# LoRA-conditioned routing kernel on one core: nine warm-ups, W's opening in halves, a full-width bias sum, the last batch by halves with its last chunks stored singly, and one product moved up

## What is computed

```python
def cond(x, adapter_mapping, W, b, lora_As, lora_Bs):      # R = 16, SCALING = 2
    base_out = jnp.einsum('bti,oi->bto', x, W) + b
    A, Bm = lora_As[adapter_mapping], lora_Bs[adapter_mapping]
    lora_h = jnp.einsum('bti,bir->btr', x, A)
    return base_out + jnp.einsum('btr,bro->bto', lora_h, Bm) * SCALING

def ffn(x, route_w, A, Bw):                                # E = 8 experts, R = 16
    logits = jnp.einsum('bsd,ed->bse', x, route_w)
    topk_v, topk_idx = jax.lax.top_k(logits, 1)
    route_weight = jax.nn.one_hot(topk_idx[..., 0], E) * topk_v
    wh = route_weight[..., None] * jnp.einsum('bsd,erd->bser', x, A)
    return jnp.einsum('bser,eor->bso', wh, Bw)

out = x + ffn(cond(x, ...), route_w, A, Bw)
```

## Time and profile before

| | us |
|---|---|
| median of 3 runs | 292.27 |
| lowest, highest | 291.97, 293.33 |
| the profiled execution | 293.44 |
| its span in the trace | 291.64 |

### The profile page before, as it was taken

How to read it: one execution, slowest core, us unless ns; L and a number is a source line. 1 busy time by engine, 2 the same in 40 slices (tenths; PEclk the granted TensorE clock), 3 DMA queues, 4 the chain that set the end, 5 groups by cost and what they waited for, 6 DMA issues and landing times.

```text
span 291.6 us, 4476 instructions
## 1 busy us (share of the span) xinstructions
PE 284.0 (97%) x1731; PEld 228.1 (78%) x1731; DVE 203.5 (70%) x238; ACT 113.3 (39%) x171; POOL 12.7 (4%) x45
## 2 busy tenths in 40 slices
PE   6999999999999999999999999999999999999992
PEld 4999999998675885788588758857885887887992
DVE  0043100067497999699789969996998898898883
ACT  0010201097685542734274355427432732432500
POOL 6200300000000000000000000000000000000000
PEclk9999999999999999999999999999999999999998
DMA  7999999999970066949967993999499679455577
GB/s 239 411 394 398 416 413 411 376 411 417 420 331 0 10 280 210 365 146 388 387 236 255 418 364 144 369 372 383 139 396 375 246 242 426 199 224 243 187 254 248
DMA packets 21352, 88.54 MB, mean 304 GB/s; under 512 B 2378, under 2 KB 8914, under 8 KB 13522
## 3 DMA queue, kind: packets, MB, share of 16 engines
q1 hardware_dynamic: 18464, 85.79, 75.8%
q10 hardware_dynamic: 2866, 2.46, 2.6%
HBM read 54.60 MB, written 33.55 MB: 302 GB/s over the span
## 4 chain that ended last, share of the span: by engine, by line
PE 89%; DVE 5%; issue 2%; DMA 1%; ACT 1%; DVEq 0%; ACTq 0%
PE bank_out L595 16%; PE bank_h L669 10%; PE bank_out L633 9%; PE bank_out L635 9%; PE bank_out L634 9%; PE bank_h L670 9%; PE bank_h L671 9%; PE bank_e L654 9%; DVE x_ring L542 3%; DVE x_lo L448 2%; DMA pt<-PT 1%; PE bank_l L609 1%; PE bank_l L595 1%; PE bank_h L595 1%; PE bank_e L595 1%
## 5 line engine op out<-in xcount | busy, mean ns | idle before, releaser
L353 ACT ACTIVATE x_hi<-x_ring 128x1024 fp32r<-128x1024 f32 (+1 forms) x72 | 68.8, 964 | 64.7 <-PE bank_h L671 64.2
L448 DVE TENSOR_TENSOR x_lo<-x_ring,x_hi 128x1024 fp32r<-128x1024 f32 (+1 forms) x72 | 79.0, 1103 | 12.3 <-ACT x_hi L353 11.2
L542 DVE TENSOR_TENSOR x_ring<-bank_out,x_ring 128x1024 f32<-128x1024 f32 (+1 forms) x72 | 79.1, 1102 | 0.7 <-PE bank_out L635 0.3
L669 PE MATMUL bank_h<-x_hi,m_hi 128*128 128x512 f32 (+1 forms) x144 | 54.1, 376 | 0.1
L633 PE MATMUL bank_out<-wh_hi,bw_hi 128*128 128x512 f32 (+1 forms) x144 | 53.3, 370 | 0.0
L670 PE MATMUL bank_h<-x_lo,m_hi 128*128 128x512 f32 (+1 forms) x144 | 53.2, 369 | 0.0
L671 PE MATMUL bank_h<-x_hi,m_lo 128*128 128x512 f32 (+1 forms) x144 | 53.2, 369 | 0.0
L635 PE MATMUL bank_out<-wh_hi,bw_lo 128*128 128x512 f32 (+1 forms) x144 | 53.2, 369 | 0.0
L634 PE MATMUL bank_out<-wh_lo,bw_hi 128*128 128x512 f32 (+1 forms) x144 | 53.2, 369 | 0.0
L595 PE MATMUL bank_out<-pt,w_ring 128*128 128x136 f32 x384 | 47.9, 287 | 1.1 <-DMA pt<-PT 1.1
L595 PEld LDWEIGHTS bank_out<-pt,w_ring 128*128 128x128 f32 x384 | 47.1, 198 | 2.2 <-DMA w_ring<-W 2.0
(11 more groups left out here) (71 smaller groups left out, 160.7 us busy)
## 6 DMA issues: line engine op xcount, KB each, us to landing
x_ring<-xT SPq DMA_DIRECT2D x32, 1024.0 KB, 7.5
outT<-x_ring SPq DMA_DIRECT2D x28, 1024.0 KB, 4.8
w_ring<-W SPq DMA_DIRECT2D x31, 512.0 KB, 10.0
outT<-x_ring SPq DMA_DIRECT2D x16, 256.0 KB, 2.6
x_ring<-loraB ACTq DMA_DIRECT2D x8, 128.0 KB, 9.8
la<-loraA ACTq DMA_DIRECT2D x8, 128.0 KB, 13.9
x_ring<-BwT SPq DMA_DIRECT2D x1, 1024.0 KB, 9.8
pt<-PT SPq DMA_DIRECT2D x3, 272.0 KB, 7.3
```

What stands on the lines that cost most here:

```text
L353: act.activation(out, in_, ACT.Copy).then_inc(done, 1)
L448: dve.tensor_tensor(out, a, b, ALU.subtract).then_inc(done, 1)
L542: dve.tensor_tensor(x, out_banks(u, j), x, ALU.add).then_inc(v_out, 1)
L669: mm(h, m_hi[:, c, :], hi, start=(c == 0), stop=False)
```

## The change

- `WARM_UP` is 9 instead of 6. The cleared tile is 128 columns wide and is read four times over for the 512 columns.
- Piece 1 of W is loaded and awaited in two halves too, like piece 0 (`HALVED` = 2). Parts 2, 3 and 4 of `pt` are issued behind the pieces 3, 6 and 9 instead of 1, 3 and 5 (`PT_AFTER`).
- ACT issues loraB's loads and the first two of loraA once piece 6 is done (`LB_AT`), not piece 2.
- `ones` has 128 columns, so the bias sum's weight is 128 x 128 and its result stands on all 128 partitions; one of them is used as before.
- The last batch lies in HBM and in the ring by halves of its tokens: its first two pieces hold the first 256 tokens of 8 chunks each, the other two the second 256 tokens. A pair of chunks of a half is then one run of 512 columns, in x and in the output.
- The stores of the very last unit are issued by SP (even pairs) and ACT (odd pairs). Its last pair is worked as two single chunks: the second one goes to bank_h, each is added by DVE on its own and stored on its own, the first by ACT, the second by SP.
- For unit 0 `weigh` is done right behind `weight`, ahead of the `x_lo` that followed it.

```diff
--- before.py
+++ after.py
...
@@ -67,11 +71,12 @@
     NWP = NWB * NWH
     PT_PARTS = [(0, 2), (2, 4), (4, 8), (8, 12), (12, 16)]
     NPT = len(PT_PARTS)
+    HALVED = 2
+    PT_AFTER = {3: 2, 6: 3, 9: 4}
     OPEN = NWB // 2
     ORDER = [(blk, part) for part in range(NWH) for blk in range(OPEN)] + [
         (blk, part) for blk in range(OPEN, NWB) for part in range(NWH)]
     DONE = [max(n for n in range(NWP) if ORDER[n][0] == blk) + 1 for blk in range(NWB)]
-    NPIECES = NB * NQ
     assert ER == P and WI == 2 * P and NWB == NP2 and NB * R == P and BIAS_ROW < GROUP
 
     ctx = ExitStack()
...
@@ -106,8 +111,8 @@
         g_a = sb("g_a", [GROUP, NB, XN], F32, phase1)
         bp = sb("bp", [P, XN], F32, phase1)
         pb = sb("pb", [1, XN], F32, phase1)
-        warm = sb("warm", [P, T], mybir.dt.bfloat16, phase1)
-        ones = sb("ones", [P, 1], F32, phase1)
+        warm = sb("warm", [P, P], mybir.dt.bfloat16, phase1)
+        ones = sb("ones", [P, P], F32, phase1)
         beats0 = sb("beats0", [P, 2, E], F32, phase1)
         phase1.close()
         e_top = sb("e_top", [2 * GROUP, T])
...
@@ -190,13 +195,19 @@
 
             eng.wait_ge(d_x[k % XRING], 16 * (k // XRING + 1))
 
+        def x_piece(u, j):
+
+            b, t0, nt = UNITS[u]
+            return NQ * b + (C * t0 + 2 * nt * j) // PIECE
+
         def x_pair(u, j):
 
-            b, t0, nt = UNITS[u]
-            k = NQ * b + 2 * j // PC
-            return x_ring[:, k % XRING, 2 * j % PC:2 * j % PC + 2, t0:t0 + nt]
-
-        WARM_UP = 6
+            nt = UNITS[u][2]
+            at = 2 * nt * j % PIECE
+            return x_ring[:, x_piece(u, j) % XRING, at:at + 2 * nt].rearrange("p (c t) -> p c t", c=2)
+
+        WARM_UP = 9
+        LB_AT = 6
         BW_AT = 19
         BP_AT = 20
 
@@ -222,6 +233,10 @@
                 return bank_out[j % 2][:, :, :]
             return bank_out[j // 2 % 2][:, j % 2, :].rearrange("p (i t) -> p i t", i=2)
 
+        def last_banks(i):
+
+            return bank_h[:, 0:UNITS[-1][2]] if i == 1 else out_banks(NU - 1, NP2 - 1)[:, 0, :]
+
         def pairs_added(u, j):
 
             if UNITS[u][2] == T:
@@ -229,6 +244,23 @@
             if UNITS[u - 1][2] == T and j < 4:
                 return NP2 * u - 1 + j // 2
             return NP2 * u + j - 3
+
+        def store_single(eng, i):
+
+            u, j = NU - 1, NP2 - 1
+            nt = UNITS[u][2]
+            at = 2 * nt * j % PIECE + i * nt
+            k = x_piece(u, j)
+            eng.wait_ge(v_out, NP2 * NU - 1 + i + 1)
+            eng.dma_start(outT[k, :, at:at + nt], x_ring[:, k % XRING, at:at + nt]).then_inc(d_last, 16)
+
+        def store_pair(eng, u, j):
+
+            nt = UNITS[u][2]
+            at = 2 * nt * j % PIECE
+            k = x_piece(u, j)
+            eng.wait_ge(v_out, NP2 * u + j + 1)
+            eng.dma_start(outT[k, :, at:at + 2 * nt], x_ring[:, k % XRING, at:at + 2 * nt]).then_inc(d_last, 16)
 
         block = ctx.enter_context(nc.Block())
 
@@ -238,9 +270,9 @@
                 if n >= WRING:
                     sp.wait_ge(t_w, n - WRING + 1)
                 blk, part = ORDER[n]
-                if n == 0:
-                    sp.dma_start(w_ring[:, 0, 0:WO // 2, :], W[blk, part, :, 0:WO // 2, :]).then_inc(d_w_first, 16)
-                    sp.dma_start(w_ring[:, 0, WO // 2:WO, :], W[blk, part, :, WO // 2:WO, :]).then_inc(d_w[0], 16)
+                if n < HALVED:
+                    sp.dma_start(w_ring[:, n, 0:WO // 2, :], W[blk, part, :, 0:WO // 2, :]).then_inc(d_w_first[n], 16)
+                    sp.dma_start(w_ring[:, n, WO // 2:WO, :], W[blk, part, :, WO // 2:WO, :]).then_inc(d_w[n], 16)
                 else:
                     sp.dma_start(w_ring[:, n % WRING, :, :], W[blk, part]).then_inc(d_w[n % WRING], 16)
 
@@ -251,17 +283,17 @@
                 elif slot in EARLY:
                     sp.wait_ge(t_bp, 1)
                     sp.wait_ge(v_bw, 1)
-                sp.dma_start(x_ring[:, slot, :, :], xT[k // NQ, k % NQ]).then_inc(d_x[slot], 16)
+                sp.dma_start(x_ring[:, slot, :], xT[k]).then_inc(d_x[slot], 16)
 
             def store(k):
                 sp.wait_ge(v_out, (k + 1) * (PC // 2))
-                sp.dma_start(outT[k // NQ, k % NQ], x_ring[:, k % XRING, :, :]).then_inc(d_out[k % XRING], 16)
+                sp.dma_start(outT[k], x_ring[:, k % XRING, :]).then_inc(d_out[k % XRING], 16)
 
 
             for n in range(NWP):
                 load_w(n)
-                if n in (1, 3, 5):
-                    k = 2 + n // 2
+                if n in PT_AFTER:
+                    k = PT_AFTER[n]
                     c0, c1 = PT_PARTS[k]
                     sp.dma_start(pt[:, c0:c1, :], PT[:, c0:c1, :]).then_inc(d_pt[k], 16)
                 if n == 7:
@@ -279,14 +311,13 @@
                 if k >= LAG and k - LAG + XRING < NPIECES:
                     load_x(k - LAG + XRING)
             for u in range(NB - 1, NU):
-                b, t0, nt = UNITS[u]
                 for j in range(NP2):
-                    sp.wait_ge(v_out, NP2 * u + j + 1)
-                    q, c = 2 * j // PC, 2 * j % PC
-                    sp.dma_start(outT[b, q, :, c:c + 2, t0:t0 + nt], x_pair(u, j)).then_inc(d_last, 16)
+                    if u < NU - 1 or j % 2 == 0:
+                        store_pair(sp, u, j)
+            store_single(sp, 1)
             for s in range(XRING):
                 sp.wait_ge(d_out[s], 16 * len(range(s, LAST, XRING)))
-            sp.wait_ge(d_last, 16 * NP2 * (NU - NB + 1))
+            sp.wait_ge(d_last, 16 * (NP2 * (NU - NB + 1) + 1))
 
         @block.gpsimd
         def _(pool):
@@ -368,13 +399,13 @@
                     act.wait_ge(t_w, NWP - WRING + j + 1)
                 elif g >= SRING:
                     act.wait_ge(t_main, g - SRING + 1)
-                x_landed(act, NQ * b + 2 * j // PC)
+                x_landed(act, x_piece(u, j))
                 copy(x_hi[:, g % SRING, :, 0:nt], x_pair(u, j), a_xhi)
 
             act.wait_ge(g_zero, ZEROED)
             for n in range(NWB):
                 if n == 0:
-                    act.wait_ge(t_w, 2)
+                    act.wait_ge(t_w, LB_AT)
                     for b in range(NB):
                         act.dma_start(lb[:, b, :, :].rearrange("p c r -> p (c r)"),
                                       loraB[bass.ds(slot[b], 1), :, :].rearrange("s p n -> p (s n)")).then_inc(d_lb, 16)
...
@@ -441,6 +472,9 @@
                 if u >= 2:
                     act.wait_ge(t_out, NP2 * (u - 1))
                 copy(wh_hi[u % 2][:, 0:nt], wh[:, 0:nt], a_wh)
+            for j in range(1, NP2 - 1, 2):
+                store_pair(act, NU - 1, j)
+            store_single(act, 0)
 
         @block.vector
         def _(dve):
@@ -554,21 +588,27 @@
                         compare(u)
                     if j == W_AT:
                         weight(u)
+                        if u == 0:
+                            weigh(u)
                     if j < SRING:
                         split_lo(u, SRING + j)
                     elif u + 1 < NU:
                         split_lo(u + 1, j - SRING)
                     if u >= 1 and 1 <= j <= NP2 - HELD[u]:
                         add_x(u - 1, j - 1)
-                weigh(u)
-                if u >= 1:
+                if u >= 1:
+                    weigh(u)
                     add_x(u - 1, NP2 - HELD[u])
                 weigh_lo(u)
                 if u >= 1:
                     for j in range(NP2 - HELD[u] + 1, NP2):
                         add_x(u - 1, j)
-            for j in range(NP2):
+            for j in range(NP2 - 1):
                 add_x(NU - 1, j)
+            for i in range(2):
+                x = x_pair(NU - 1, NP2 - 1)[:, i, :]
+                dve.wait_ge(t_out, NP2 * NU - 1 + i + 1)
+                dve.tensor_tensor(x, last_banks(i), x, ALU.add).then_inc(v_out, 1)
 
         @block.tensor
         def _(pe):
@@ -579,12 +619,12 @@
                 blk, part = ORDER[n]
                 if part == 0 and blk >= OPEN:
                     pe.wait_ge(v_m, M_LOTS[blk - OPEN if blk < OPEN + 2 else blk - 2])
-                halves = ((0, WO // 2), (WO // 2, WO)) if n == 0 else ((0, WO),)
+                halves = ((0, WO // 2), (WO // 2, WO)) if n < HALVED else ((0, WO),)
                 for o0, o1 in halves:
                     if o1 == WO:
                         pe.wait_ge(d_w[n % WRING], 16 * (n // WRING + 1))
                     else:
-                        pe.wait_ge(d_w_first, 16)
+                        pe.wait_ge(d_w_first[n], 16)
                     for i in range(2):
                         bank = w_banks(blk)[i][0][:, 0:PN] if len(w_banks(blk)) == 2 else w_banks(blk)[0][0][:, i, 0:PN]
                         for o in range(o0, o1):
@@ -599,7 +639,7 @@
 
             pe.wait_ge(v_warm, 1)
             for _ in range(WARM_UP):
-                mm(bank_h[:, :], warm[:, 0:P], warm[:, :], start=True, stop=True)
```

(22 more changed lines are left out.)

30 lines of the change are left out of this document (17 added, 13 removed).

## The result

| | before | after |
|---|---|---|
| median of the paired runs (6 each) | 292.68 | 290.50 |
| lowest, highest | 291.97, 293.33 | 290.11, 291.54 |
| the profiled execution | 293.44 | 290.62 |
| its span | 291.64 | 288.83 |

The ratio is 0.9928, with a 95% interval from 0.9904 to 0.9951: the change makes the kernel 2.2 us faster. In the profiled executions the span falls by 2.81 us. It falls in four places, which I take in order of time (together 2.75 us; the other 0.06 is not placed).

A forecast was written before the change was run, and what follows sets the result against it. It took TensorE to bound the kernel (busy 284.0 of 291.64 us). Gains of 2.2 + 0 + 0 + 0.1 + 0.2 + 1.6 = 4.1 took the profiled 293.44 to 289.34, less 0.34 to 289.0 us; range 287.6 to 290.8.

The forecast's parts named there:

- the second rival: Last stores: 2 KB rows no faster than 1 KB, end gains 0.4 instead of 1.6, 290.2 us; chance 0.18.
- Nine warm-ups, 2.2: Opening: warm-ups without a rest ahead of W's first product bring the full clock earlier; gain 2.2 us (0 to 2.5).
- The step to 5.5: Opening: full clock comes 4.5 us behind the start of unbroken work, so at 5.5 us, leaving a cost of 0.25.
- The rival that the clock isn't hastened: Opening: the rest had no part, the rise stays near 9.5 us; 291.2 us, chance 0.12.
- W in halves, `pt` reordered, loraB later, 0 and cover: Opening loads: no gain themselves, but W arrives in time for a fast PE; 0 (0 to -0.5), loraB 0.
- The third rival: loraB's loads land too late for bank_l's product and PE stands; slower, 301 us at twice the 18 us, chance 0.03.
- Bias sum, 0.1: Bias sum on 128 columns: its two records, 0.32 us, run at the common pitch; gain 0.1 us (0 to 0.1).
- `weigh(0)`, 0.2: Behind batch 0: `weigh` ahead of `x_lo` ends PE's wait for DVE, 3.79 to 3.57 us; gain 0.2 (0 to 0.22).
- The end, 1.6: Last batch by halves, stores on two queues, last pair in two: span ends at 290.0 us; gain 1.6 (0.3 to 2.1).
- The fit of 378 GB/s: Last stores: times fitted to 1 KB and 8 KB rows give 378 GB/s at 2 KB, just above the 370 made.
- The landing "2.1 to 2.6": Last store: takes 2.1 to 2.6 us to land, from a lone 256 KB's 2.1, with perhaps 384 KB in flight ahead.
- The 0.34 taken off: From profiled 289.34 to median 289.0 us: 0.34 of the 1.17 us between profiled and unprofiled executions deducted.

The follow-up runs named there:

- a_six: The changed kernel with six warm-ups again instead of nine; median 292.50 us, ratio 0.9977.
- a_late: The changed kernel with six warm-ups held back by five small DVE clears so that they meet W's first product; median 291.26 us, ratio 0.9946.
- a_one: The changed kernel with the bias sum on one column of ones again, timed once; 26.47 us from bank_l's product to the first short one.
- b_nine: The kernel before with nine warm-ups instead of six and nothing else; median 292.33 us, ratio 0.9983.
- a_sp: The changed kernel with all stores of the last unit issued by SP, none by ACT; median 291.00 us, ratio 0.9925.
- a_rows1k: The changed kernel with the last batch laid out as before, so its stores have rows of 1 KB; median 291.31 us, ratio 0.9941.
- a_whole: The changed kernel with its last pair added and stored at once, no single chunks; median 290.33 us, ratio 0.9919.
- a_weigh: The changed kernel with `weigh` of unit 0 back behind the `x_lo`, timed once; 3.78 us from the short to the long products.
- a_pt: The changed kernel with only W's piece 0 in halves, and `pt` and loraB issued as before; median 290.99 us, ratio 0.9932.
- a_many: The changed kernel with 72 warm-ups of 64 columns and a weight of 32 columns instead of nine of 512; median 290.16 us, ratio 0.9909.
- a_best: The changed kernel with 68 small warm-ups (64 columns, a weight of 32) and the last pair whole; median 290.36 us, ratio 0.9925.
- a_fine: The changed kernel with 36 warm-ups of 128 columns instead of 9 of 512; median 290.63 us, ratio 0.9924.

## Why the prediction was right, and where it was wrong

The time, 290.50, lies in the range (287.6 to 290.8), and the kernel is faster, as forecast; it is 1.5 above the forecast of 289.0. The forecast's own terms reached to 290.0 only; the range holds 290.50 by the part that it gave the second rival. On the profiled execution the sum said 4.1 and 2.82 came. Term by term:

- **Nine warm-ups, 2.2: 1.91 measured.** The direction and the main cause are right: a_six and a_late show that the break ahead of W does it and not the amount of work, though breaks of up to 0.39 us did no harm. The step to 5.5 is wrong in kind: it took the time from the start of unbroken work to the rise as fixed, 4.5 us, and it was 4.9 in the kernel after, 3.7 in a_late, 3.4 in a_one and 5.9 in b_nine. The prediction put the full clock at 5.5, and it came at 5.87. In the six executions with just this opening (after, a_sp, a_rows1k, a_whole, a_one, a_weigh) it came anywhere from 4.36 to 7.01 us, and W's work got 1.4 to 2.3 us ahead of the kernel before (bank_h's first product starts at 12.12 us there and at 9.82 to 10.68 here). So the size of the term is one draw out of that spread, and the forecast's 2.2 lies inside it. The rival that the clock isn't hastened has fallen.
- **W in halves, `pt` reordered, loraB later, 0 and cover.** Right in kind: in its profile the kernel after waits for none of them behind its first product. The place was only half right: in a_pt it was piece 7 that came late, and when the clock rose early, in a_one, it was piece 2, cover and all. The third rival, loraB too late, has fallen; bank_l's product didn't wait.
- **Bias sum, 0.1: 0.29.** The step that failed is the one that looked at the two records alone. a_one shows 0.20 more behind them.
- **`weigh(0)`, 0.2: 0.22.** Right, with a_weigh at 0.21.
- **The end, 1.6: 0.33.** This is the mis-sized term, and nearly all of the miss in the span: 1.3 of 1.35 us. Three steps of it failed. The fit of 378 GB/s for rows of 2 KB gave too little for undisturbed stretches (398 to 410), but it was taken for the whole end, and 281 to 283 us had 236 and 299. The landing "2.1 to 2.6" was read off the lone stores of before; the last store took 3.7, since there was still a backlog ahead of it and one engine lagged. And such a lag, of 0.8 us, was in the trace of before as well, behind 290.0, and the prediction took it for part of an ordinary landing. With it the forecast of 2.9 us for the end would have been 3.7. a_many and a_best remove most of it and measure 3.61 and 3.24; what then remains over 2.9 I put down to the dip and the backlog, which no run parts. Nor is the 0.33 us itself firm. The same stores gave ends of 4.03 to 4.07 in a_one, a_weigh and a_pt, but 4.58 and 4.61 in a_six and a_late, as long as the 4.49 and 4.64 of the old ones in before and b_nine.
- **To the median.** The 0.34 taken off on the way to the median was 0.12: 290.62 against 290.50. The profiled execution of before stood 0.76 above the median of the six runs, so of the 2.82 us in the profiles 2.2 are left in the medians.

The second rival, rows of 2 KB no faster than rows of 1 KB, gave 290.2, nearest to what was measured, and the prediction's own test (an end of 4 us or more) pointed to it, with 4.16. Half of it holds. The rate doesn't: 398 to 410 against 343 to 347 GB/s contradict the 512 B of the Trainium skill's page "DMA: Bandwidth & Descriptors", section Specifications. Its effect nearly does: over the four us from 281 it was 331 against 330, over five 344 against 333. A test by the length of the end couldn't tell slow rows from a dip or from a late engine; the rate by stretches and the number of engines at work could.

Open stays what makes the dip. Every run with rows of 2 KB but a_fine has it at the same place, and a_rows1k hasn't, so it goes with those rows or with their place in HBM; a_sp shows that two queues aren't needed for it. In a_fine, where SP's long issue had let the backlog drain (176 GB/s from 280 to 281), the next two us had 348 and 346. Open is also which part of the end's edits won the 0.33 us. a_sp speaks against the second queue and a_whole against the single chunks; what is left are SP's long issue, the halves' order and the spread between executions. The long issue isn't abolished by the new stores: a_six has the same ones, and its row in the view of outT shows one of 1.31 us,

```profile
L263 SPq DMA_DIRECT2D outT<-x_ring x12: 332/332/1312, 272.9 to 285.7; - x12
```

a_late one of 1.34 and a_fine one of 1.47.

## What to carry to other kernels

Let warm-ups reach up to the first real product: a stand of 0.4 us between them did no harm here, one of 0.64 us cost 1.4 to 2.0 us in the median. The size of the single warm-up counts little. Even so the clock rose at times up to 2.7 us apart with the same code, so compare such kernels over many executions and not by one profile. When a store's landing bounds the end, count the DMA engines that are still at work in its last microsecond: one alone, a share of 0.06, is no matter of bandwidth, and a fetch of instructions in the last microseconds can be moved by some dozens of instructions far ahead. Don't cost a transfer rate from its best stretch; look at one-microsecond stretches in the phase where the backlog stands.

## What the runs showed of the hardware

- A fetch of instructions of 16 KB keeps one DMA engine busy for 0.9 to 2.1 us. Where it came 6.7 to 8.4 us before the end, one engine was alone at work at the end for 0.6 to 1.5 us; where it came 9.3 (a_fine), 13.3 (a_best) or 15.2 us ahead (a_many), for 0.1 us at most. The fetch comes earlier when PE has more instructions ahead of it.
- Stores of 2 KB rows reached 398 to 410 GB/s and, at a full busy share too, fell to 236 for one us; stores of 1 KB rows kept to 314 to 351 (a_rows1k).
- A lone store of 256 KB landed in 2.4 us with rows of 2 KB, and in 2.1 to 2.2 with rows of 1 KB.
- The full clock came at different times in executions with the same opening: at 4.36 (a_one), 5.67 (a_whole), 5.87 (after), 5.98 (a_weigh), 6.84 (a_sp) and 7.01 us (a_rows1k), by the trace's record of the clock and by the pace of TensorE's records. With 0.64 and 1.08 us of rest ahead of W it came at 9.79 and 9.60, with rests of 0.20 and 0.39 us at 6.24 (a_pt) and 5.50 (a_many).
- A float32 product with a weight of one column costs 0.29 us more than one of 128 columns, two thirds of it in the products behind it (26.47 against 26.18 us from bank_l's product to the first short one, in before and a_one against after).
- `pt` landed between 3.50 and 4.53 us behind its issue, with the same queues ahead of it (a_six and a_many).
